# A causal mask moved from a TensorE matmul to VectorE's score copy, with three PSUM banks each for scores and transposes

## The chip, the cores and the metric

The kernel runs on one core of one Trainium2 chip. The metric is the device time of one launch in microseconds (us), as the median over runs. Engines are called PE or TensorE (matmuls), DVE or VectorE, ACT or ScalarE, POOL or GpSimd, and SP, which issues the DMAs.

## What is computed

One transformer block in fp32: adaptive layer norm, causal attention with 16 heads of 128 over 2048 tokens of 512 features, output projection and residual, then a gated feed-forward part with 4-bit weights. The change lies in attention alone:

```python
k = jnp.einsum('ihd,bpd->biph', W_K, x)     # x: the normalised, modulated input
q = jnp.einsum('ihd,bpd->biph', W_Q, x)
v = jnp.einsum('ihd,bpd->biph', W_V, x)
scores = jnp.einsum('biph,biqh->biqp', k, q)
mask = jnp.tril(jnp.ones((pos, pos), dtype=x.dtype))
masked = scores * mask - jnp.float32(10000000000.0) * (1.0 - mask)
attn = jax.nn.softmax(masked / jnp.sqrt(jnp.float32(d_head)), axis=-1)
z = jnp.einsum('biqp,biph->biqh', attn, v)
out = jnp.einsum('df,bqf->bqd', W_O, z_flat)
```

## The kernel before

Every fp32 product is made of three fp32r matmuls on split operands, hi*hi, lo*hi and hi*lo (`split_matmul`, L189 to L191); the splits are made as they are copied out of PSUM, the high part by ScalarE, the low part by VectorE. The program runs in stages with a barrier between them: `prologue` (layer norm, to 57.7 us), `attention` (58.0 to about 1701 us), `output_projection`, `gate_up`, `down`.

`attention` goes through the heads one after the other; heads 1 to 14 run in loops with one body, heads 0 and 15 are written out. A head has 16 row tiles i of 128 queries. In row i the keys come in chunks c of 512, i // 4 + 1 of them, the last as wide as the diagonal reaches (128 to 512 columns); a head has 40 chunks. The steps of a chunk, by the letters that the orders use:

- S i.c (PE, `scores`): negated and scaled scores of the chunk into a bank of `ps_s`. For the last chunk of a row a bf16 matmul against the identity adds the mask (`causal`, 128x128, a large positive number over the diagonal) to the last 128 columns (L816). The narrowest chunk, of rows 0, 4, 8 and 12, is computed 256 columns wide.
- C i.c (DVE, `copy_scores`): copy to `probs` (two rows of buffer) with the minimum of each row of the chunk; after the last chunk of a row a small reduction (L964) takes the minimum over the chunks' minima.
- E i (ACT, `exponent`): one exponential over the row with that minimum as bias, and its sum.
- T i.u (PE, `transposes`): up to four 128x128 transposes into a bank of `ps_t`. H i.u (ACT) and L i.u (DVE) copy it out as high and low parts.
- Z b.u (PE, `pv`): values times probabilities for a pair of rows; Y b (ACT) copies the result, SP stores it.
- P and U are the projections of K, Q, V and the transposition of V (W), in a single bank `ps_p`, so each must be copied out by ACT and then DVE before the next begins. N, G and R handle the reciprocals of the sums. X (DVE) and nine POOL instructions for each of three pieces a head decode the 4-bit weights in heads 0 to 10.

Three tables, `PE_ORDER`, `ACT_ORDER` and `DVE_ORDER`, set the order of these steps on the three engines by hand. A step with "-" belongs to the previous head, one with "+" to the next; the last head leaves out those with "+". Waits are semaphores: S waits until the bank it writes was copied (`row_copied`), T until its bank's low part was taken (`t_lo`), E for the row minimum. Of the eight PSUM banks, `ps_s` has 4, `ps_t` 2, `ps_z` and `ps_p` 1 each.

On POOL, `split_weights` splits the next head's weights after this head's last projection of the same kind, and in the last head `split_wo` splits W_O into the space of the normalised input, which is free once PV3 of the last head is done (`hT_used`); 16 pairs of instructions (L746, L749).

Of the kernel before, what the change touches and what calls it, by code (L numbers as in the profile page):

```python
# [136 lines left out]
PT_SLOTS = 5  # L137

# [101 lines left out]
def adaln_kernel(nc, x, w_qkv, w_o, gu_packed, gu_scales, dn_packed, dn_scales, c_cols, w_mod, out):  # L240
    with ExitStack() as whole:
# [52 lines left out]
def prologue(nc, ph, start, x, w_qkv, c_cols, w_mod, ident, ident_bf, gate_a, gate_b, shift_a, scale_a,  # L294
# [82 lines left out]
    def _(pool):  # L377
# [10 lines left out]
        pool.wait_ge(start.consts, 1)  # L388
        nc.gpsimd.affine_select(out=start.causal[:, :], in_=start.zeros[:, :], compare_op=ALU.is_ge, fill=MASKED,
# [141 lines left out]
def attention(nc, ph, start, hbm, w_qkv, w_o, gu_packed, gu_scales, dn_packed, dn_scales, ident, ident_bf,  # L531
# [16 lines left out]
    z = sb("z", [P, ZBUF, 2 * P], F32)  # L548
    cmin = sb("cmin", [P, 2, NB], F32)
# [221 lines left out]
    def _(pe):  # L771
# [29 lines left out]
        def scores(h, i, c):  # L801
# [71 lines left out]
    def _(act):  # L873
# [14 lines left out]
        def transposed_hi(h, i, u):  # L888
# [46 lines left out]
    def _(dve):  # L935
# [15 lines left out]
        def copy_scores(h, i, c):  # L951
# [7 lines left out]
            least = rmin[:, i % 2:i % 2 + 1] if nch == 1 else cmin[:, i % 2, c:c + 1]  # L959
# [554 lines left out]
```

## Time and profile before

| | |
|---|---|
| runs | 2215.63 us median of 3 (2215.61 to 2218.49) |
| profiled execution | 2216.7 us, its span 2214.6 us |
| TensorE busy | 2142.3 us (97%) |
| VectorE busy | 1333.9 us (60%) |
| ScalarE busy | 1075.6 us (49%) |
| POOL busy | 718.9 us (32%) |
| DMA | mean 55 GB/s |
| transposition of the sums' reciprocals (L853), once a head | starts at 182.4 us in the first, 1697.4 us in the last |

The profile is of one execution. A matmul's record is longer than the step from one matmul to the next, since they are pipelined: what a matmul costs in a dense stream is the distance between starts, and a busy share near 100% says only that no gap is visible. VectorE's copy with a minimum is two records: the pass and a short read of the accumulator (DVE_READ_ACCUMULATOR).

### The profile page before, as it was taken

What the parts mean: (1) busy time and instruction counts of PE and PEld (TensorE: products, weight loads), DVE (VectorE), ACT (ScalarE), POOL (GpSimd) and SP (SyncE); (2) the same over time, 40 slices, a digit from 0 to 9 for tenths busy, and PEclk for the clock granted to TensorE, in tenths of its full rate; (3) what the DMA queues carried; (4) which work ended last, traced back from release to release, by engine and by line L of the source; (5) the groups of instructions that cost most, each with busy time, mean ns of one, the idle gap of its engine ahead of it and who ended that gap; (6) DMA issues with size and microseconds to landing.
All of it is one profiled execution on the core that took longest, in us unless ns stands there. A gap on an engine that the chain in (4) does not pass through costs nothing. (4 is left out here: it accounts for less than half of the span.)

```text
span 2214.6 us, 37536 instructions
## 1 busy us (share of the span) xinstructions
PE 2142.3 (97%) x12561; PEld 1838.4 (83%) x12561; DVE 1333.9 (60%) x2998; ACT 1075.6 (49%) x2006; POOL 718.9 (32%) x545
## 2 busy tenths in 40 slices
PE   6899999999999999999999999999997899899899
PEld 3688889888888888888888888888886788788687
DVE  7364646556565646465565546464554577699865
ACT  4354545454554545454545545454544333588511
POOL 3333242525153333425250101010015444388400
PEclk9999999999999999999999999999999999999999
DMA  5111010111110110101110000000004677111121
GB/s 204 36 44 37 32 33 31 33 33 33 45 38 29 43 36 31 33 31 33 33 33 32 19 18 21 14 21 12 22 27 138 206 238 236 59 39 39 43 67 66
DMA packets 84003, 122.78 MB, mean 55 GB/s; under 512 B 9315, under 2 KB 49891, under 8 KB 83939
## 3 DMA queue, kind: packets, MB, share of 16 engines
q1 hardware_dynamic: 81635, 117.76, 16.3%
q10 hardware_dynamic: 2304, 4.20, 0.5%
q8 instruction: 36, 0.59, 0.1%
q14 instruction: 28, 0.23, 0.0%
HBM read 87.97 MB, written 33.95 MB: 55 GB/s over the span
## 5 line engine op out<-in xcount | busy, mean ns | idle before, releaser
L960 DVE TENSOR_SCALAR_CACHE_REDUCE probs<-ps_s 128x512 f32<-128x512 f32 (+3 forms) x640 | 371.2, 607 | 263.2 <-PE ps_t L827 116.4
L971 DVE TENSOR_TENSOR pT_lo<-ps_t,pT_hi 128x512 fp32r<-128x512 f32 (+3 forms) x640 | 368.9, 605 | 248.6 <-ACT pT_hi L892 247.3
L892 ACT ACTIVATE pT_hi<-ps_t 128x512 fp32r<-128x512 f32 (+3 forms) x640 | 318.6, 531 | 230.5 <-PE ps_t L827 229.6
L903 ACT ACTIVATE probs<-probs,rmin 128x128 f32<-128x128 f32 (+15 forms) x256 | 308.1, 1204 | 137.2 <-DVE rmin L964 111.9
L189 PE MATMUL ps_z<-pT_hi,v_hi 128*128 128x256 f32 (+1 forms) x1152 | 333.4, 289 | 0.0
L189 PE MATMUL ps_p<-hT_hi,w_hi 128*128 128x512 f32 x768 | 319.9, 417 | 8.7 <-PEq L269 4.1
L191 PE MATMUL ps_z<-pT_hi,v_lo 128*128 128x256 f32 (+1 forms) x1152 | 324.7, 282 | 0.0
L190 PE MATMUL ps_z<-pT_lo,v_hi 128*128 128x256 f32 (+1 forms) x1152 | 324.7, 282 | 0.0
L827 PE MATMUL ps_t<-ident,probs 128*128 128x128 f32 x2176 | 309.1, 273 | 4.5 <-DVE pT_lo L971 2.5
L191 PE MATMUL ps_p<-hT_hi,w_lo 128*128 128x512 f32 x768 | 303.1, 395 | 0.0
L190 PE MATMUL ps_p<-hT_lo,w_hi 128*128 128x512 f32 x768 | 301.1, 392 | 0.0
L827 PEld LDWEIGHTS ps_t<-ident,probs 128*128 128x128 f32 x2176 | 254.0, 140 | 39.9 <-DVE pT_lo L971 2.8
L189 PE MATMUL ps_s<-kT_hi,qT_hi 128*128 128x512 f32 (+2 forms) x640 | 262.1, 409 | 0.0
L191 PE MATMUL ps_s<-kT_hi,qT_lo 128*128 128x512 f32 (+2 forms) x640 | 233.8, 365 | 0.0
L190 PE MATMUL ps_s<-kT_lo,qT_hi 128*128 128x512 f32 (+2 forms) x640 | 233.4, 365 | 0.0
L190 PEld LDWEIGHTS ps_z<-pT_lo,v_hi 128*128 128x128 f32 x1152 | 220.2, 191 | 2.7
L189 PEld LDWEIGHTS ps_z<-pT_hi,v_hi 128*128 128x128 f32 x1152 | 220.0, 191 | 2.7
L191 PEld LDWEIGHTS ps_z<-pT_hi,v_lo 128*128 128x128 f32 x1152 | 219.7, 191 | 0.0
L233 POOL TENSOR_TENSOR w_hi<-w_raw,zeros 128x512 fp32r<-128x512 f32 x48 | 50.0, 1042 | 481.5 <-PE ps_p L191 481.5
L727 POOL TENSOR_TENSOR turn<-zeros 128x1 f32<-128x1 f32 x33 | 6.4, 193 | 552.1 <-DVE words L990 552.1
L189 PEld LDWEIGHTS ps_p<-hT_hi,w_hi 128*128 128x128 f32 x768 | 146.4, 191 | 33.2 <-issue 4.9
L191 PEld LDWEIGHTS ps_p<-hT_hi,w_lo 128*128 128x128 f32 x768 | 144.8, 189 | 33.5
(136 smaller groups left out, 3813.7 us busy)
## 6 DMA issues: line engine op xcount, KB each, us to landing
scratch_zT<-z SPq DMA_DIRECT2D x256, 64.0 KB, 1.6
o_z<-scratch_zT SPq DMA_DIRECT2D x31, 512.0 KB, 7.2
o_scales<-scratch_recips SPq DMA_DIRECT2D x31, 512.0 KB, 8.0
w_raw<-in_w_qkv SPq DMA_DIRECT2D x16, 768.0 KB, 4.5
p_wmod<-in_w_mod SPq DMA_DIRECT2D x6, 1024.0 KB, 10.6
words<-in_gu_packed SPq DMA_DIRECT2D x44, 128.0 KB, 3.1
scratch_wgu<-deq_a SPq DMA_DIRECT2D x22, 256.0 KB, 2.0
g_codes<-scratch_wgu SPq DMA_DIRECT2D x11, 512.0 KB, 3.4
```

The lines of the kernel that those rows point to most:

```text
L189: nc.tensor.matmul(dst, stat[0], mov[0], start=start, stop=False)
L190: nc.tensor.matmul(dst, stat[0], mov[1], start=False, stop=False)
L191: return nc.tensor.matmul(dst, stat[1], mov[0], start=False, stop=stop)
L233: nc.gpsimd.tensor_tensor(st.w_hi[:, m, :], st.w_raw[:, m, :], st.zeros[:, 0:1].to_broadcast([P, DC * DH]), ALU.add) \
L727: then(nc.gpsimd.tensor_tensor(turn[:, :], zeros[:, 0:1], zeros[:, 0:1], ALU.add))
L827: last = nc.tensor.transpose(ps_t[:, n % 2, (k - 4 * u) * P:(k - 4 * u + 1) * P], probs[:, i % 2, k * P:(k + 1) * P], ident[:, :])
L892: nc.scalar.activation(pT[0][:, slot, i % 2, 0:w], ps_t[:, (chunks_before(i) + u) % 2, 0:w], ACT.Copy).then_inc(t_hi, 1)
L903: nc.scalar.activation(probs[:, i % 2, 0:w], probs[:, i % 2, 0:w], ACT.Exp, bias=rmin[:, i % 2:i % 2 + 1], scale=-1.0, accum_out=sums[:, i ...
L960: nc.vector.tensor_scalar(probs[:, i % 2, c * BT:c * BT + w], ps_s[:, at % NB, 0:w], 1.0, None, ALU.mult, ALU.min, accum_out=least).then_i ...
L971: nc.vector.tensor_tensor(pT[1][:, slot, i % 2, 0:w], ps_t[:, (chunks_before(i) + u) % 2, 0:w], pT[0][:, slot, i % 2, 0:w].bitcast(F32), A ...
```

## The change

The mask matmul is gone. `causal` becomes fp32, 512 columns wide, 384 of zeros and the 128x128 mask at the end, and the last chunk of each row is copied by a `tensor_tensor_reduce`: scores plus the last w columns of `causal`, with the minimum. The row minimum is chained: each chunk's copy starts from the minimum of the one before (`least_before`), so the small reduction L964 goes, and each copy but a row's first waits for the one before it (`row_copied`). Ahead of each `tensor_tensor_reduce` stands a one-column memset (`lead`), and the waits are on it. The narrowest chunk is computed 128 wide. `ps_s` and `ps_t` have 3 banks each; a bank counter that does not divide 40 starts anew with each head (`freed`). The three orders are new.

```diff
+def freed(h, n, banks):
+
+    last = n - banks if n >= banks else max(m for m in range(CHUNKS) if m % banks == n % banks) - CHUNKS
+    return CHUNKS * h + last + 1
 PE_ORDER = """
-    S0.0 T15.2- Z7.0- T15.3- T0.0 PW0 Z7.1- Z7.2- PK1.0 PK1.1 PK1.2 PK1.3 Z7.3- N0- S1.0 S2.0 PQ1.0 PQ1.1 T1.0 PQ1.2
+    S0.0 S1.0 Z7.1- PW0 T0.0 T1.0 Z7.2- PK1.0 PK1.1 PK1.2 PK1.3 Z7.3- S2.0 N0- PQ1.0 PQ1.1 PQ1.2 PQ1.3 S3.0 Z0.0 T2.0
...
 ACT_ORDER = """
-    E0 H15.3- H0.0 UW0 UK1 G0- Y7- E1 E2 H1.0 UQ1 H2.0 Y0 E3 UV1 H3.0 UW1 E4 Y1 E5 H4.0 UK2 H4.1 H5.0 H5.1 E6 UQ2 E7
+    E0 E1 UW0 H0.0 H1.0 UK1 G0- Y7- E2 UQ1 Y0 H2.0 E3 E4 UV1 H3.0 H4.0 H4.1 UW1 Y1 E5 E6 UK2 H5.0 H5.1 H6.0 UQ2 E7 Y2
...
 DVE_ORDER = """
-    C0.0 L15.2- L15.3- L0.0 UW0 UK1 C1.0 C2.0 X0 L1.0 UQ1 L2.0 C3.0 C4.0 L3.0 UW1 C4.1 C5.0 C5.1 L4.0 C6.0
+    C0.0 C1.0 X0 UW0 L0.0 L1.0 UK1 C2.0 UQ1 C3.0 L2.0 C4.0 C4.1 L3.0 L4.0 L4.1 C5.0 C5.1 UW1 C6.0 C6.1 X1 UK2 L5.0
...
+S_BANKS = 3
+T_BANKS = 3
...
-                    causal=sb("causal", [P, P], BF16, both), zeros=sb("zeros", [P, P], F32, both),
+                    causal=sb("causal", [P, BT], F32, both), zeros=sb("zeros", [P, P], F32, both),
...
-            if not (isinstance(h, int) and CHUNKS * h + at < NB):
-                pe.wait_ge(row_copied, CHUNKS * h + at - NB + 1)
-            n = BT if c < b else max(r + 1, 2) * P
+            if not (is_at(h, 0) and at < S_BANKS):
+                pe.wait_ge(row_copied, freed(h, at, S_BANKS))
+            n = BT if c < b else (r + 1) * P
             k = [part[:, c * BT:c * BT + n] for part in kT]
-            diagonal = c == b
-            last = split_matmul(nc, ps_s[:, at % NB, 0:n], q, k, True, True)
-            if diagonal:
-                last = nc.tensor.matmul(ps_s[:, at % NB, r * P:(r + 1) * P], ident_bf[:, :], causal[:, :],
-                                        start=False, stop=True, skip_group_check=True)
-            last.then_inc(scores_ready, 1)
+            split_matmul(nc, ps_s[:, at % S_BANKS, 0:n], q, k, True, True).then_inc(scores_ready, 1)
...
-            if not (isinstance(h, int) and CHUNKS * h + n < 2):
-                pe.wait_ge(t_lo, CHUNKS * h + n - 1)
+            if not (is_at(h, 0) and n < T_BANKS):
+                pe.wait_ge(t_lo, freed(h, n, T_BANKS))
...
-            if n_chunks(i) == 1:
-                act.wait_ge(row_copied, CHUNKS * h + chunks_before(i) + 1)
-            else:
-                act.wait_ge(min_ready, (NT - TPB) * h + i - TPB + 1)
+            act.wait_ge(row_copied, CHUNKS * h + chunks_before(i + 1))
...
-            least = rmin[:, i % 2:i % 2 + 1] if nch == 1 else cmin[:, i % 2, c:c + 1]
-            nc.vector.tensor_scalar(probs[:, i % 2, c * BT:c * BT + w], ps_s[:, at % NB, 0:w], 1.0, None,
-                                    ALU.mult, ALU.min, accum_out=least).then_inc(row_copied, 1)
-            if nch > 1 and c == nch - 1:
-                dve.wait_ge(row_copied, CHUNKS * h + chunks_before(i) + nch)
-                nc.vector.tensor_reduce(rmin[:, i % 2:i % 2 + 1], cmin[:, i % 2, 0:nch], AX_X, ALU.min) \
-                  .then_inc(min_ready, 1)
+            least = rmin[:, i % 2:i % 2 + 1] if c == nch - 1 else cmin[:, i % 2, c:c + 1]
+            least_before = cmin[:, i % 2, c - 1:c] if c else None
+            if c:
+                dve.wait_ge(row_copied, CHUNKS * h + at)
+            out = probs[:, i % 2, c * BT:c * BT + w]
+            if c < nch - 1:
+                ins = nc.vector.tensor_scalar(out, ps_s[:, at % S_BANKS, 0:w], 1.0, least_before,
+                                              ALU.mult, ALU.min, accum_out=least)
+            else:
+                nc.vector.memset(lead[:, i % 2:i % 2 + 1], 0.0)
+                ins = nc.vector.tensor_tensor_reduce(out=out, in0=ps_s[:, at % S_BANKS, 0:w], in1=causal[:, BT - w:BT],
+                                                     scale=1.0, scalar=least_before if c else 3e38, op0=ALU.add, op1=ALU.min,
+                                                     accum_out=least)
+            ins.then_inc(row_copied, 1)
```

TensorE at the start of a loop head, before: S0.0 with its mask, then a bank of transposes of the previous head's last row (T15.2-) and Z7.0-.

```order
L189 MATMUL ps_s<-kT_hi,qT_hi 128x256
L190 MATMUL ps_s<-kT_lo,qT_hi 128x256
L191 MATMUL ps_s<-kT_hi,qT_lo 128x256
L816 MATMUL ps_s<-causal,ident_bf 128x128
L825 ISA
L827 MATMUL ps_t<-ident,probs 128x128 x4
L833 ISA
L837 ISA
L189 MATMUL ps_z<-pT_hi,v_hi 128x256
```

The same place of the change: S0.0 and S1.0, then Z7.1-.

```order
L197 MATMUL ps_s<-kT_hi,qT_hi 128x128
L198 MATMUL ps_s<-kT_lo,qT_hi 128x128
L199 MATMUL ps_s<-kT_hi,qT_lo 128x128
L819 REGISTER_ALU
L197 MATMUL ps_s<-kT_hi,qT_hi 128x256
L198 MATMUL ps_s<-kT_lo,qT_hi 128x256
L199 MATMUL ps_s<-kT_hi,qT_lo 128x256
L840 ISA
L841 ISA
L197 MATMUL ps_z<-pT_hi,v_hi 128x256
```

Two rows' scores now stand together at the head's start, the first of them 128 columns wide and neither with a mask matmul; T15.2- and T15.3- have moved into the head that they belong to.

TensorE at the end of row 12 in the change (S12.2, S12.3, PW3, T11.0 to T11.2, S13.0); register instructions stand between the steps.

```order
L197 MATMUL ps_s<-kT_hi,qT_hi 128x512
L198 MATMUL ps_s<-kT_lo,qT_hi 128x512
L199 MATMUL ps_s<-kT_hi,qT_lo 128x512
L819 REGISTER_ALU
L197 MATMUL ps_s<-kT_hi,qT_hi 128x128
L198 MATMUL ps_s<-kT_lo,qT_hi 128x128
L199 MATMUL ps_s<-kT_hi,qT_lo 128x128
L787 REGISTER_ALU
L796 MATMUL ps_p<-ident,vT 128x128 x4
L826 REGISTER_ALU
L831 MATMUL ps_t<-ident,probs 128x128 x12
L819 REGISTER_ALU
```

All four chunks of row 12 now follow each other, and all of row 11's transposes; before, S12.2 and S12.3 stood behind T10.2, and a projection came behind S12.3.

VectorE at the start of a loop head, before: C1.0, C2.0 and the unpacking of a weight piece (X0) come behind UK1.

```order
L948 TENSOR_TENSOR kT_lo<-ps_p,kT_hi 128x512
L957 REGISTER_ALU
L960 TENSOR_SCALAR probs,rmin<-ps_s 128x256
L957 REGISTER_ALU
L960 TENSOR_SCALAR probs,rmin<-ps_s 128x384
L984 ISA
L985 TENSOR_TENSOR words<-words,nib_shift 128x512
```

In the change (L969 is the `tensor_tensor_reduce`, its second row the read of the accumulator):

```order
L968 MEMSET lead 128x1
L969 ISA probs,rmin<-ps_s,causal 128x128
L969 ISA rmin 128x1
L957 REGISTER_ALU
L968 MEMSET lead 128x1
L969 ISA probs,rmin<-ps_s,causal 128x256
L969 ISA rmin 128x1
L991 ISA
L992 TENSOR_TENSOR words<-words,nib_shift 128x512
```

C0.0 and C1.0 open the head together, each as a memset, a masked copy and an accumulator read, and X0 is third.

## Rows read from the trace of the kernel before

**Rows 1.** windows, a loop head and the last: us, busy us by engine, granted clock, DMA.
```profile
284.02:385.59 101.57, 101.57 (x651) 89.22 (x651) 58.66 (x155) 50.87 (x97) 38.01 (x31) 1.00 0.11 35
1604.47:1697.38 92.91, 90.44 (x594) 79.33 (x594) 51.87 (x139) 48.00 (x89) 36.66 (x32) 1.00 0.17 49
```

**Rows 2.** TensorE's waits at transposes, whole run (us in total, times, longest).
```profile
PE ps_t L827 <- DVE pT_lo L971: 2.5, 4, 1.0
PE ps_t L827 <- ACT probs L903: 2.1, 1, 2.1
```

**Rows 3.** TensorE's timeline round a mask matmul with scores behind it (start, us).
```profile
1675.33 0.34 PE L191 MATMUL ps_s<-kT_hi,qT_lo 128*128 128x384 f32 x1
1675.51 0.23 PE L816 MATMUL ps_s<-causal,ident_bf 128*128 128x128 bf16 x1
1675.54 0.47 PE L189 MATMUL ps_s<-kT_hi,qT_hi 128*128 128x512 f32 x1
1675.86 0.39 PE L190 MATMUL ps_s<-kT_lo,qT_hi 128*128 128x512 f32 x1
1676.09 0.40 PE L191 MATMUL ps_s<-kT_hi,qT_lo 128*128 128x512 f32 x1
```

**Rows 4.** TensorE's timeline, a mask matmul with transposes behind it.
```profile
405.52 0.23 PE L816 MATMUL ps_s<-causal,ident_bf 128*128 128x128 bf16 x1
405.59 0.28 PE L827 MATMUL ps_t<-ident,probs 128*128 128x128 f32 x1
```

**Rows 5.** TensorE's timeline, a 256-column triple's first matmul and the mask behind it.
```profile
578.47 0.28 PE L189 MATMUL ps_s<-kT_hi,qT_hi 128*128 128x256 f32 x1
...
578.83 0.23 PE L816 MATMUL ps_s<-causal,ident_bf 128*128 128x128 bf16 x1
```

**Rows 6.** TensorE's timeline, a 128-column triple and the last matmul of attention.
```profile
1697.10 0.22 PE L189 MATMUL ps_z<-pT_hi,v_hi 128*128 128x128 f32 x1
...
1697.38 0.27 PE L853 MATMUL ps_z<-ident,recips 128*16 128x128 f32 x1
```

**Rows 7.** VectorE's groups by shape (out<-in, count, busy us, mean ns, idle before).
```profile
L971 DVE TENSOR_TENSOR pT_lo<-ps_t,pT_hi 128x512 fp32r<-128x512 f32 x448 | 296.4, 685 | 229.4 <-ACT pT_hi L892 228.2
L960 DVE TENSOR_SCALAR_CACHE_REDUCE probs<-ps_s 128x512 f32<-128x512 f32 x448 | 295.6, 687 | 170.7 <-PE ps_t L827 116.4 <-PE ps_s L191 52.3
L971 DVE TENSOR_TENSOR pT_lo<-ps_t,pT_hi 128x128 fp32r<-128x128 f32 x64 | 18.0, 282 | 2.4 <-ACT pT_hi L892 2.4
L964 DVE TENSOR_REDUCE rmin<-cmin 128x1 f32<-128x4 f32 x64 | 10.1, 157 | 2.2
```

**Rows 8.** VectorE's timeline over copies without and a reduction with an own wait.
```profile
1683.73 0.68 DVE L960 TENSOR_SCALAR_CACHE_REDUCE probs<-ps_s 128x512 f32<-128x512 f32 x1
1684.34 0.69 DVE L960 TENSOR_SCALAR_CACHE_REDUCE probs<-ps_s 128x512 f32<-128x512 f32 x1
1684.95 0.08 DVE L960 DVE_READ_ACCUMULATOR probs<-ps_s 128x1 f32 x1
1685.07 0.16 DVE L964 TENSOR_REDUCE rmin<-cmin 128x1 f32<-128x4 f32 x1
```

**Rows 9.** timeline of the first head, transposed values to the next projection.
```profile
74.00 0.60 PE L787 MATMUL ps_p<-ident,vT 128*128 128x128 f32 x4
75.26 0.69 DVE L948 TENSOR_TENSOR v_lo<-ps_p,v_hi 128x512 fp32r<-128x512 f32 x1 [0.47 <-ACT v_hi L880]
76.01 0.59 PE L189 MATMUL ps_p<-hT_hi,w_hi 128*128 128x512 f32 x1 [1.41 <-DVE v_lo L948]
```

**Rows 10.** ScalarE's group of the 256-column exponential.
```profile
L903 ACT ACTIVATE probs<-probs,rmin 128x256 f32<-128x256 f32 x16 | 8.2, 512 | 4.9 <-DVE probs L960 4.9
```

**Rows 11.** timeline, POOL's first and last W_O split, then the next stage's first load.
```profile
1651.83 1.04 POOL L746 TENSOR_TENSOR hT_hi<-w_raw,zeros 128x512 fp32r<-128x512 f32 x1 [99.23 <-PE ps_p L191]
...
1688.47 1.28 POOL L749 TENSOR_TENSOR hT_lo<-w_raw,hT_hi 128x512 fp32r<-128x512 f32 x1
...
1701.01 0.34 SPq L1085 DMA_DIRECT2D o_z<-scratch_zT  x1
```

More of the change, by code:

```diff
@@ L75 @@
-    S12.0 S12.1 T10.2 S12.2 S12.3 PQ0.0+ S13.0 T11.0 S13.1 T11.1 S13.2 S13.3 T11.2 Z5.0 S14.0 T12.0 T12.1 Z5.1 Z5.2
-    T12.2 T12.3 S14.1 S14.2 S14.3 S15.0 S15.1 S15.2 T13.0 T13.1 S15.3 PQ0.1+ PQ0.2+ PQ0.3+ T13.2 Z6.0 T13.3 PK0.0+
-    PK0.1+ PK0.2+ PK0.3+ T14.0 T14.1 Z6.1 Z6.2 T14.2 T14.3 Z6.3 PV0.0+ PV0.1+ T15.0 T15.1 PV0.2+ PV0.3+
+    S0.0 S1.0 Z7.1- PW0 T0.0 T1.0 Z7.2- PK1.0 PK1.1 PK1.2 PK1.3 Z7.3- S2.0 N0- PQ1.0 PQ1.1 PQ1.2 PQ1.3 S3.0 Z0.0 T2.0
+    S4.0 S4.1 PV1.0 PV1.1 PV1.2 PV1.3 T3.0 T4.0 T4.1 S5.0 S5.1 PW1 Z1.0 S6.0 S6.1 S7.0 PK2.0 PK2.1 PK2.2 PK2.3 T5.0
@@ new lines @@
+    T5.1 T6.0 S7.1 PQ2.0 PQ2.1 PQ2.2 PQ2.3 Z2.0 Z2.1 PV2.0 PV2.1 PV2.2 PV2.3 T6.1 T7.0 T7.1 PW2 S8.0 S8.1 S8.2 Z3.0
+    PK3.0 S9.0 S9.1 S9.2 PK3.1 Z3.1 PK3.2 PK3.3 T8.0 T8.1 T8.2 S10.0 S10.1 PQ3.0 PQ3.1 PQ3.2 PQ3.3 S10.2 T9.0 T9.1
+    T9.2 S11.0 S11.1 S11.2 Z4.0 T10.0 T10.1 T10.2 Z4.1 Z4.2 PV3.0 PV3.1 PV3.2 PV3.3 S12.0 S12.1 S12.2 S12.3 PW3 T11.0
+    T11.1 T11.2 S13.0 S13.1 S13.2 S13.3 Z5.0 T12.0 T12.1 Z5.1 Z5.2 T12.2 T12.3 T13.0 S14.0 S14.1 S14.2 PQ0.0+ PQ0.1+
+    S14.3 PQ0.2+ PQ0.3+ T13.1 T13.2 T13.3 S15.0 S15.1 S15.2 S15.3 Z6.0 Z6.1 Z6.2 T14.0 T14.1 T14.2 Z6.3 PK0.0+ PK0.1+
@@ L78 @@
+    T14.3 T15.0 T15.1 PK0.2+ PK0.3+ T15.2 T15.3 Z7.0 PV0.0+ PV0.1+ PV0.2+ PV0.3+
 """
 ACT_ORDER = """
-    E0 H15.3- H0.0 UW0 UK1 G0- Y7- E1 E2 H1.0 UQ1 H2.0 Y0 E3 UV1 H3.0 UW1 E4 Y1 E5 H4.0 UK2 H4.1 H5.0 H5.1 E6 UQ2 E7
-    H6.0 Y2 H6.1 UV2 H7.0 H7.1 UW2 Y3 UK3 E8 E9 UQ3 H8.0 H8.1 UV3 H8.2 H9.0 UW3 H9.1 H9.2 E10 H10.0 H10.1 Y4 E11
-    H10.2 H11.0 E12 H11.1 H11.2 H12.0 H12.1 E13 Y5 H12.2 H12.3 E14 H13.0 H13.1 UQ0+ H13.2 H13.3 UK0+ H14.0 H14.1
-    E15 H14.2 H14.3 Y6 H15.0 H15.1 UV0+ H15.2
+    E0 E1 UW0 H0.0 H1.0 UK1 G0- Y7- E2 UQ1 Y0 H2.0 E3 E4 UV1 H3.0 H4.0 H4.1 UW1 Y1 E5 E6 UK2 H5.0 H5.1 H6.0 UQ2 E7 Y2
@@ L88 @@
-    L8.0 L8.1 C10.0 C10.1 L8.2 L9.0 UW3 C10.2 C11.0 L9.1 L9.2 X2 C11.1 C11.2 L10.0 L10.1 C12.0 C12.1 C12.2 C12.3
-    L10.2 L11.0 C13.0 L11.1 L11.2 C13.1 C13.2 L12.0 L12.1 C13.3 C14.0 C14.1 C14.2 C14.3 L12.2 L12.3 L13.0
-    L13.1 UQ0+ L13.2 C15.0 L13.3 C15.1 C15.2 C15.3 UK0+ L14.0 L14.1 R0 L14.2 L14.3 L15.0 L15.1
+    C0.0 C1.0 X0 UW0 L0.0 L1.0 UK1 C2.0 UQ1 C3.0 L2.0 C4.0 C4.1 L3.0 L4.0 L4.1 C5.0 C5.1 UW1 C6.0 C6.1 X1 UK2 L5.0
+    L5.1 L6.0 C7.0 C7.1 UQ2 L6.1 L7.0 UW2 L7.1 C8.0 C8.1 C8.2 C9.0 C9.1 C9.2 X2 UK3 L8.0 L8.1 L8.2 C10.0 C10.1 C10.2
@@ L91 @@
+    UQ3 L9.0 C11.0 C11.1 L9.1 L9.2 C11.2 L10.0 L10.1 L10.2 C12.0 C12.1 C12.2 C12.3 UW3 L11.0 C13.0 C13.1 C13.2 L11.1
+    L11.2 C13.3 L12.0 L12.1 L12.2 L12.3 L13.0 C14.0 C14.1 C14.2 C14.3 C15.0 L13.1 L13.2 L13.3 C15.1 C15.2 C15.3 UQ0+
+    R0 L14.0 L14.1 L14.2 L14.3 L15.0 L15.1 UK0+ L15.2 L15.3
 """
@@ L387, in _ @@
         nc.gpsimd.memset(start.zeros[:, :], 0.0).then_inc(start.consts, 1)
[L388 to L389 removed]
+        nc.gpsimd.memset(start.causal[:, 0:BT - P], 0.0).then_inc(start.consts, 1)
+        pool.wait_ge(start.consts, 2)
+        nc.gpsimd.affine_select(out=start.causal[:, BT - P:BT], in_=start.zeros[:, :], compare_op=ALU.is_ge, fill=MASKED,
                                 base=0, pattern=[[-1, P]], channel_multiplier=1).then_inc(start.consts, 1)
```

24 lines of the change are left out of this document (11 added, 13 removed).

## Prediction

> **What bounds the kernel now.** I read the page's first part, then the windows of single heads, then the waits of TensorE, then its timeline. The windows show a head as a fixed period: 101.57 us, of which TensorE is busy 101.57, VectorE 58.66, ScalarE 50.87, POOL 38.01, at a granted clock of 1.00, the upper of the two levels (2.4 GHz) [rows 1]. A busy share alone could hide short waits. The waits say that there are none in the loop: at transposes TensorE waited 4.6 us in the whole run, five times, once in the first head and four times in the last [rows 2], whose window has 90.44 busy of 92.91 us [rows 1]. So in heads 1 to 14 time is the sum of the distances between matmul starts. What leaves that stream is gained, and what VectorE takes on costs nothing until TensorE has to wait for it. The other stages have no edit.
>
> **What leaves TensorE.** *The mask matmul.* Its record says 0.23 us, which is not its cost. With scores behind it: from L191 at 1675.33 to the second matmul of the next step at 1675.86 are 0.53 us [rows 3]. Without it these would be 0.18 (a 384-column matmul to what follows it) and 0.23 (512 columns, 1675.86 to 1676.09), 0.41 together. The mask costs 0.12 us. With a transpose behind it, it costs its own step, 0.07 us [rows 4]. By the order before, 11 of the 16 in a head are followed by fp32r matmuls and 5 by transposes (rows 0, 6, 7, 10, 13): 11 x 0.12 + 5 x 0.07 = 1.67 us a head.
>
> *The narrower chunk.* A 256-column triple takes 0.36 us (578.47 to 578.83) [rows 5], one of 128 columns 0.28 (1697.10 to 1697.38, the same split matmuls in Z) [rows 6]. Four rows a head: 0.32 us. The Trainium skill, "TensorE: Matmul & The Clock Gate", section "Back-to-back issue gap", gives N/2.4 + 2.5 ns for a warm matmul, thus 0.056 us for 128 columns and 0.109 for 256, and by it the saving would be 0.16 us a triple, 0.64 a head. The section on LDWEIGHTS of that page gives 0.107 us for a load of 128 columns, which would hold a narrow matmul up, and the row's 0.28 for three goes with this. I take the row.
>
> Together 1.99 us a head. All 16 heads have the same 16 masks and four narrow chunks: 31.8 us. The other matmuls are the same in number and width; their new order costs nothing by itself, since a change from transposes to fp32r matmuls moves a start but not the sum of two steps.
>
> **What VectorE takes on.** The trace has no `tensor_tensor_reduce`. The nearest rows are L971, two inputs, one in PSUM and one in SBUF, 685 ns for 512 columns and 282 for 128, and L960, one input with a minimum, 687 for 512 [rows 7]. They agree, so I price the new one like them, nothing on top. Below that it can't go, as no VectorE row that reads PSUM is faster; above, see the rivals. The memset has one column: between the accumulator read, 0.08 us, and L964, 0.16 [rows 7, 8]; I take 0.1, 16 times 1.6 us. Chaining costs overlap: copies that wait for nothing start 0.61 us apart (1683.73, 1684.34), while an instruction that waits for the copy before it starts 0.73 behind it (1685.07) [rows 8], so 24 chained copies cost up to 24 x 0.12 = 2.9 us. Twelve L964 go; behind one the next instruction would have followed some 0.2 us sooner: 2.2 us. VectorE ends near 61 us of a head of 99.6. The sum is hidden by TensorE; only its place in the order could matter.
>
> **Where TensorE could now wait.** I laid the new orders out with the steps above and looked at the short distances.
>
> (a) Head start. From S0.0: S0.0 0.28, S1.0 0.36, Z7.1 four triples 1.44, PW0 four transposes of 0.11 (0.60 for four records, 0.27 for one [rows 6, 9]) to 2.52, T0.0, T1.0 at 2.63. E1 must be done by then. S1.0 ends near 0.8, its copy near 1.4 with memset and read, E1 takes 0.51 [rows 10] behind E0: about 2.05. Slack 0.58. PK1.0 wants to start at 2.63 + 0.22 + 1.44 = 4.29; from the start of PW to the next projection are 2.01 us (74.00 to 76.01, ScalarE and VectorE both free) [rows 9], so 2.08 + 2.01 = 4.09. Slack 0.20.
>
> (b) S12.3 with three banks reuses that of S12.0 and comes after S12.0 to S12.2, 3 x 0.69 = 2.08. The copy C12.0 starts near 0.9, and is done at 1.65. Slack 0.4; S13.3 and S15.3 have the same distance. Ahead of C13.0 VectorE has C12.1 to C12.3 (0.73 each, the last narrow), UW3 and L11.0: it starts near 4.85 and ends at 5.6, and S13.3 is due at 2.08 + 0.28 + 0.44 + 12 x 0.11 + 2.08 = 6.2. Slack 0.57. With two banks for transposes the order before had to keep such distances there; a third loosens them.
>
> (c) Last head. POOL's splits of W_O start when PV3 is through and take 1651.83 to 1689.75, 37.9 us; TensorE ends at 1697.4 and the next stage begins at 1701.01, 3.6 later [rows 6, 11]. In the new order PV3 comes later: behind it TensorE has rows 12 to 15, transposes of rows 11 to 15, Z5 to Z7 and PW3, 33.2 us, and waits as before for want of the next head's projections (T14.3 behind E15, T15.2 and T15.3), 3.3. So the next stage is due 36.5 + 3.6 = 40.1 after PV3, POOL is done at 38. Cover shrinks from 11 to 2 us and still holds; without it each us would show once. I put the changes of both written-out heads at nothing, within 1 us.
>
> No slack is negative, so the steady head is 101.57 - 1.99 = 99.6.
>
> **The sum.** The profiled execution took 2216.7 us, its span 2214.6. 2216.7 - 31.8 = 2184.9. The median of the runs is 1.1 below the profiled one: 2184.
>
> **Rivals.**
>
> *Half rate.* The Trainium skill, "Vector Engine (DVE) Microarchitecture Reference", section "Points that are easy to get wrong", says that a two-source operation with an accumulator halves its throughput if both sources are in SBUF and not bf16. Here one is in PSUM, and L971 shows no loss [rows 7], but L971 accumulates nothing. As a mechanism: the slope of L971 is (685 - 282) / 384 = 1.05 ns a column, so half rate adds 0.13 us at 128 columns and 0.54 at 512. At (a) that is 0.13 + 0.27 against 0.58, at (b) 0.13 against 0.57. Only small waits come of it, 0 to 0.5 us a head: 2184 to 2192. Chance 0.12.
>
> *Waits of queues.* My distances are estimates of some 0.2 us, and (a) has that much. Three to five places late by 0.1 to 0.2 give up to 0.8 us a head: to 2196. Chance 0.13. If instead the new order lost all that the matmuls gave, 1.7 to 2.3 us a head, the time would be within 2211 to 2220. For it speaks that ScalarE and VectorE now meet longer runs of scores and transposes; against it, VectorE's 39 us of room a head. Chance 0.05.
>
> *A dear reduce (slower).* `tensor_tensor_reduce` is no row here, and could have a fixed price F on top. At the head's start two stand in line: 2F - 0.58 us lost; at (b) F - 0.57. Both reach the 1.99 gained at F = 1.05. At 1.5 a head loses 3.35, net 1.36, and the time is 2215.6 + 16 x 1.36 = 2237. Against it: the shortest VectorE rows, 0.08 and 0.16 us [rows 7, 8], leave no room for a fixed microsecond in what that engine does here. Chance 0.05.
>
> **How the numbers follow.** The likeliest case, 0.65, is 2184 within 2180 (all 16 masks worth 0.12, and no waits in the first head's start) and 2188. Half rate and small waits add 0.25 up to 2196. The range 2180 to 2196 leaves out 0.1. Faster by over 0.2% (4.4 us, about what a measurement of this kernel tells from no change): 0.90; within it 0.05; slower 0.05.
>
> **What would show it.** The last matmul of two following heads should stand 99.6 us apart, with TensorE's starts 0.23 apart from the last chunk's third matmul to the next step. L969 should read near 0.69 us for 512 columns, the memset 0.1, a chained copy start 0.73 behind the one before. TensorE's waits in the loop should be none; those for `ps_s` would be new, and so would POOL as the last before the next stage. The prediction is wrong if the windows of single heads show TensorE less than busy, above all at T1.0, PK1.0 or S13.3, or if L969 has a price of its own.

## The result, and the profile after

The changed kernel takes 2183.13 us (median of 4 runs, 2178.68 to 2183.67), the kernel before 2215.62 (median of 4, 2212.49 to 2218.49). The ratio is 0.9849, 95% interval 0.9831 to 0.9868: 1.5% faster. The forecast was 2184 within 2180 to 2196. The profiled execution took 2183.67 us, its span 2181.7.

The windows of a loop head and of the last head, cut as in [rows 1] from one transposition of the reciprocals to the next, columns as there:

```profile
core 0: us, PE busy (x) PEld busy (x) DVE busy (x) ACT busy (x) POOL busy (x), PEclk, DMA share, GB/s
280.09:379.59 99.50, 99.50 (x635) 89.51 (x633) 59.79 (x158) 49.94 (x97) 38.00 (x32) 1.00 0.11 36
...
1573.59:1664.43 90.84, 88.90 (x570) 79.89 (x569) 51.86 (x137) 45.95 (x86) 35.98 (x32) 0.98 0.18 50
```

A loop head went from 101.57 to 99.50 us, 2.07 less, and TensorE still has no gap in it. Fourteen of them give 29.0 us, the last head 2.1 (92.91 to 90.84), the first 1.4 (124.44 to 123.08), and attention begins 0.5 sooner. That is 33.0, and the spans differ by 32.9.

In the loop it does not matter where in a head the mark stands; in the two written-out heads it does. The new order has S1.0, S2.0 and T1.0 ahead of the mark (N0-), the old one behind it. TensorE's timeline at the start of the last head's window, before and after:

```profile
1604.47 0.27 PE L853 MATMUL ps_z<-ident,recips 128*16 128x128 f32 x1
1604.50 0.36 PE L189 MATMUL ps_s<-kT_hi,qT_hi 128*128 128x256 f32 x1
...
1605.62 0.47 PE L189 MATMUL ps_p<-hT_hi,w_hi 128*128 128x512 f32 x1
```

```profile
1573.02 0.39 PE L197 MATMUL ps_s<-kT_hi,qT_hi 128*128 128x384 f32 x1
...
1573.59 0.27 PE L857 MATMUL ps_z<-ident,recips 128*16 128x128 f32 x1
1573.61 0.48 PE L197 MATMUL ps_p<-hT_hi,w_hi 128*128 128x512 f32 x1
```

S1.0 and S2.0 took 1.12 us there, T1.0 some 0.2 more: about 1.3 us of work moved from the last window into the first. Neither 2.1 nor 1.4 can be read alone. Their sum can: the two heads gave 3.4 us together, where the forecast had 4.0.

TensorE's waits inside attention, the whole run. Between 183 and 1573 us the list is empty.

```profile
PE ps_p L197 <- DVE kT_lo L948: 2.3, 2, 1.4
PE ps_t L831 <- DVE pT_lo L978: 1.6, 1, 1.6
PE ps_p L197 <- DVE qT_lo L945: 1.5, 1, 1.5
PE ps_t L831 <- ACT probs L903: 1.3, 2, 1.2
PE ps_p L197 <- DVE v_lo L948: 0.8, 1, 0.8
PE ps_s L197 <- DVE probs L965: 0.2, 1, 0.2
```

All are in the two written-out heads, as in [rows 2]. The wait on a bank of scores (`ps_s`) is new and is 0.2 us in the last head. The four waits on `pT_lo` of the last head have become one of 1.6.

VectorE's groups in the loop head, by shape (names, shapes, count, busy us, mean ns, idle before), to read beside [rows 7]:

```profile
L965 DVE TENSOR_SCALAR_CACHE_REDUCE probs<-ps_s,cmin 128x512 f32<-128x512 f32 x12 | 9.0, 750 | 1.4
L965 DVE TENSOR_SCALAR_CACHE_REDUCE probs<-ps_s 128x512 f32<-128x512 f32 x12 | 8.2, 686 | 5.6 <-PE ps_s L199 5.5
...
L969 DVE CUSTOM_DVE_ANT_0 probs<-ps_s,causal,cmin 128x512 f32<-128x512 f32 x3 | 2.2, 750 | 0.0
...
L969 DVE CUSTOM_DVE_ANT_0 probs<-ps_s,causal,cmin 128x128 f32<-128x128 f32 x3 | 1.1, 351 | 0.0
...
L968 DVE MEMSET lead<- 128x1 f32 x16 | 0.9, 59 | 1.2
L969 DVE CUSTOM_DVE_ANT_0 probs<-ps_s,causal 128x512 f32<-128x512 f32 x1 | 0.7, 685 | 0.0
...
L969 DVE CUSTOM_DVE_ANT_0 probs<-ps_s,causal 128x128 f32<-128x128 f32 x1 | 0.3, 287 | 2.8 <-issue 2.8
```

The reader is to compare rows with and without `cmin` among the inputs. Without it the new reduce takes 685 ns for 512 columns and 287 for 128, which is what L971 took. With it, the chained minimum as its start, both the plain copy and the reduce take 64 to 65 ns more. In VectorE's timeline two chained copies in a row (start, us) stand 0.88 apart, where unchained ones stand 0.61 apart [rows 8]:

```profile
348.52 0.75 DVE L965 TENSOR_SCALAR_CACHE_REDUCE probs<-ps_s,cmin 128x512 f32<-128x512 f32 x1
...
349.40 0.75 DVE L965 TENSOR_SCALAR_CACHE_REDUCE probs<-ps_s,cmin 128x512 f32<-128x512 f32 x1
```

### The profile page after: what moved, and what is told of

The parts are those of the page before. It is cut to its first block and busy times, and to the rows that moved or that the text cites. A ratio compares the mean times of both kernels' runs of the same rounds, so it can differ in the third digit from the quotient of the medians.

```text
span 2181.7 us, 37262 instructions
## 1 busy us (share of the span) xinstructions
PE 2112.4 (97%) x12305; PEld 1845.1 (85%) x12305; DVE 1353.7 (62%) x3062; ACT 1059.6 (49%) x2006; POOL 719.3 (33%) x546
## 5 line engine op out<-in xcount | busy, mean ns | idle before, releaser
L978 DVE TENSOR_TENSOR pT_lo<-ps_t,pT_hi 128x512 fp32r<-128x512 f32 (+3 forms) x640 | 360.3, 605 | 219.9 <-ACT pT_hi L895 219.7
L895 ACT ACTIVATE pT_hi<-ps_t 128x512 fp32r<-128x512 f32 (+3 forms) x640 | 304.9, 534 | 87.5 <-PE ps_t L831 86.2
L197 PE MATMUL ps_z<-pT_hi,v_hi 128*128 128x256 f32 (+1 forms) x1152 | 326.4, 283 | 0.0
L197 PE MATMUL ps_p<-hT_hi,w_hi 128*128 128x512 f32 x768 | 309.6, 403 | 8.6 <-PEq L277 4.1
L831 PE MATMUL ps_t<-ident,probs 128*128 128x128 f32 x2176 | 278.9, 274 | 3.1 <-DVE pT_lo L978 1.6
L197 PE MATMUL ps_s<-kT_hi,qT_hi 128*128 128x512 f32 (+3 forms) x640 | 244.1, 381 | 0.2 <-DVE probs L965 0.2
L199 PE MATMUL ps_s<-kT_hi,qT_lo 128*128 128x512 f32 (+3 forms) x640 | 233.1, 364 | 0.0
L198 PE MATMUL ps_s<-kT_lo,qT_hi 128*128 128x512 f32 (+3 forms) x640 | 232.7, 364 | 0.0
L965 DVE TENSOR_SCALAR_CACHE_REDUCE probs<-ps_s 128x512 f32<-128x512 f32 x192 | 131.7, 686 | 88.4 <-PE ps_s L199 87.0
L198 PEld LDWEIGHTS ps_p<-hT_lo,w_hi 128*128 128x128 f32 x768 | 145.7, 190 | 24.3
```

What stands on the lines that cost most here:

```text
L197: nc.tensor.matmul(dst, stat[0], mov[0], start=start, stop=False)
L198: nc.tensor.matmul(dst, stat[0], mov[1], start=False, stop=False)
L199: return nc.tensor.matmul(dst, stat[1], mov[0], start=False, stop=stop)
L831: last = nc.tensor.transpose(ps_t[:, n % T_BANKS, (k - 4 * u) * P:(k - 4 * u + 1) * P], probs[:, i % 2, k * P:(k + 1) * P], ident[:, :])
L965: ins = nc.vector.tensor_scalar(out, ps_s[:, at % S_BANKS, 0:w], 1.0, least_before, ALU.mult, ALU.min, accum_out=least)
L978: nc.vector.tensor_tensor(pT[1][:, slot, i % 2, 0:w], ps_t[:, (chunks_before(i) + u) % T_BANKS, 0:w], pT[0][:, slot, i % 2, 0:w].bitcast(F ...
```

## The experiments

Loop heads are read as periods between the reciprocals' transpositions; inside one profile nearly all repeat within some 0.05 us, and two profiles of the changed kernel have 99.50 and 99.47, so a single profile resolves what a median of whole runs does not.

### Taking the parts of the change apart

**The mask matmul alone, in the old orders.** Nothing takes its place, so the diagonal blocks stay unmasked.

```diff
-            if diagonal:
-                last = nc.tensor.matmul(ps_s[...], ident_bf[:, :], causal[:, :], start=False, stop=True, ...)
```

> The kernel before with the 16 mask matmuls of a head left out and nothing put in their place, so that the diagonal blocks are not masked; everything else, the orders and the 4 and 2 banks too, stays. My theory: a mask matmul costs TensorE 0.12 us ahead of scores or projections and 0.07 ahead of transposes, 11 and 5 times a head, 1.67 us. The loop head goes from 101.57 to 99.90, the time by 26.7 us to 2189. Rival one: the cost is the 0.23 us of its record, 3.7 us a head: 97.9 and 2157. Rival two: it costs only its 128 columns at the full clock, 0.056 us, 0.9 a head: 100.7 and 2201. If the changed kernel owes something to its orders beyond the instructions, this run and the wide-chunk run together explain less than the 2.07 us a head that it gained.

Measured: 2187.54 us (2184.54 to 2190.30), ratio 0.9873 [0.9853, 0.9892]. A loop head:

```profile
282.60:382.33 99.73, 99.73 (x636) 89.00 (x635) 58.50 (x155) 50.84 (x97) 38.10 (x31) 1.00 0.11 36
```

The mask costs 1.84 us a head in the old orders, 0.115 us each over all 16, where 1.67 was expected. Neither rival holds (3.7 and 0.9).

**The narrow chunk undone.**

```diff
-            n = BT if c < b else (r + 1) * P
+            n = BT if c < b else max(r + 1, 2) * P
```

> The changed kernel with one part undone: the last chunk of scores is again at least 256 columns wide (four rows a head). My theory: 0.08 us a triple of matmuls, 0.32 a head; the loop head goes from 99.50 to 99.82, the time by 5.1 us to 2188. Rival: time of a triple in proportion to its columns, 0.16 us each, 0.64 a head: 100.14 and 2193. If nothing changes (99.50), TensorE is not what sets the head at these places.

Measured: 2184.72 us (2184.11 to 2186.55), ratio 0.9862 [0.9845, 0.9879]. The narrow chunk is worth 0.17 us a head and not 0.32. A loop head:

```profile
282.49:382.16 99.67, 99.67 (x635) 89.66 (x634) 59.81 (x158) 49.92 (x97) 38.02 (x32) 1.00 0.11 36
```

TensorE's timeline shows where the rest went. First the changed kernel, row 8's last chunk and the Z behind it, then the same place with 256 columns:

```profile
309.42 0.22 PE L197 MATMUL ps_s<-kT_hi,qT_hi 128*128 128x128 f32 x1
309.48 0.28 PE L198 MATMUL ps_s<-kT_lo,qT_hi 128*128 128x128 f32 x1
309.59 0.27 PE L199 MATMUL ps_s<-kT_hi,qT_lo 128*128 128x128 f32 x1
309.70 0.33 PE L197 MATMUL ps_z<-pT_hi,v_hi 128*128 128x256 f32 x1
309.87 0.28 PE L198 MATMUL ps_z<-pT_lo,v_hi 128*128 128x256 f32 x1
```

```profile
311.88 0.28 PE L197 MATMUL ps_s<-kT_hi,qT_hi 128*128 128x256 f32 x1
311.99 0.28 PE L198 MATMUL ps_s<-kT_lo,qT_hi 128*128 128x256 f32 x1
312.11 0.28 PE L199 MATMUL ps_s<-kT_hi,qT_lo 128*128 128x256 f32 x1
312.23 0.28 PE L197 MATMUL ps_z<-pT_hi,v_hi 128*128 128x256 f32 x1
312.35 0.28 PE L198 MATMUL ps_z<-pT_lo,v_hi 128*128 128x256 f32 x1
```

The triple itself went from 0.35 to 0.28 us, as forecast. But the first matmul behind a narrow triple keeps its place for 0.17 us instead of 0.12. From the first score matmul to the second Z matmul are 0.45 us against 0.47: most of the gain of the triple is given back one step later.

**Orders and banks alone, under the old instructions.**

The kernel before, with the changed kernel's `PE_ORDER`, `ACT_ORDER` and `DVE_ORDER`, `S_BANKS = 3`, `T_BANKS = 3` and `freed`.

> The kernel before (mask matmul on TensorE, minimum by a reduction of its own, last chunk at least 256 wide) with only the three new orders and the 3 and 3 banks. The old orders under the changed instructions gave a loop head of 100.32 us with two waits of 0.29 and 0.33 us at transposes. My theory now: those waits come from the shorter TensorE stream against two banks for transposes; the orders give nothing to the old instructions except some 12 fewer changes between transposes and fp32r matmuls at about 5 ns. Loop head 101.45 to 101.55, time 2213 to 2216. Rival: the orders are worth 0.8 us a head whatever the instructions: 100.75, time 2203. Third: the old instructions wait in the new orders, loop head over 101.7.

Measured: 2209.52 us (2208.15 to 2212.54, 10 runs), ratio 0.9978 [0.9969, 0.9987]. A loop head:

```profile
284.09:385.41 101.32, 101.32 (x651) 89.77 (x651) 58.86 (x154) 49.95 (x97) 37.98 (x32) 1.00 0.11 35
```

With the old instructions the orders give 0.25 us a head; the expectation was 0.06 from fewer changes between transposes and fp32r steps, the rival 0.8. No wait was removed (there was none before), so it is the sum of the distances that shrank. The new order has 121 distances from transpose to transpose in a head instead of 109, thus 12 changes fewer. But those changes are not what the 0.25 is made of. The two runs without the mask, this section's first (99.73) and the one with the wide chunk (99.67), have the same 634 matmuls a head, one in the old order and one in the new, and neither has a wait in the loop, so their different work on VectorE is hidden. Between them the orders give 0.06 us, 0.005 for each of the 12 changes. The other 0.19 is there only while the mask matmuls are: with them 101.57 to 101.32, without 99.73 to 99.67. The masks as a whole cost 1.84 us in the old order and 1.65 in the new. What makes this difference stays open; by the prediction's prices the new order, with 12 masks ahead of fp32r matmuls and 4 ahead of transposes instead of 11 and 5, would cost 0.05 more.

The last head's window fell from 92.91 to 89.95. About 1.3 of these 2.96 us are the steps that stand ahead of the mark now (592 matmuls in the window before, 582 here), and TensorE's gaps in it fell from 2.5 to 1.0.

**The new instructions in the old orders, with 4 and 2 banks.**

> The changed kernel with the three orders of before and with the banks of before (4 for scores, 2 for transposed chunks); mask on VectorE, chained minimum and 128-column chunk stay. My theory: the gain comes from the instructions that leave TensorE, the orders give nothing by themselves, so the loop head is 99.50 to 99.7 and the time 2180 to 2188. Rival: with two banks for transposed chunks and VectorE's new work in the old places, TensorE waits somewhere in each head, and the new orders are what keeps the gain: loop head 100 to 101.6, time 2191 to 2216. The waits of TensorE in the loop (none, or at scores or transposes) tell them apart.

Measured: 2196.77 us (2196.31 to 2199.87), ratio 0.9919 [0.9901, 0.9937]. The rival holds. Window, TensorE's waits from 200 to 1500 us, then VectorE's and TensorE's timelines at one of the two places:

```profile
282.68:383.00 100.32, 100.02 (x635) 88.75 (x635) 59.25 (x159) 50.89 (x97) 38.09 (x31) 1.00 0.11 35
```

```profile
PE ps_t L831 <- DVE pT_lo L978: 2.6, 14, 0.3
```

```profile
339.29 0.69 DVE L965 TENSOR_SCALAR_CACHE_REDUCE probs<-ps_s 128x512 f32<-128x512 f32 x1 [0.88 <-PE ps_t L831]
...
340.12 0.75 DVE L965 TENSOR_SCALAR_CACHE_REDUCE probs<-ps_s,cmin 128x512 f32<-128x512 f32 x1
...
341.01 0.75 DVE L965 TENSOR_SCALAR_CACHE_REDUCE probs<-ps_s,cmin 128x512 f32<-128x512 f32 x1
...
341.94 0.35 DVE L969 CUSTOM_DVE_ANT_0 probs<-ps_s,causal,cmin 128x128 f32<-128x128 f32 x1
...
342.22 0.55 DVE L978 TENSOR_TENSOR pT_lo<-ps_t,pT_hi 128x384 fp32r<-128x384 f32 x1
```

```profile
342.31 0.40 PE L199 MATMUL ps_s<-kT_hi,qT_lo 128*128 128x512 f32 x1
342.83 0.33 PE L831 MATMUL ps_t<-ident,probs 128*128 128x128 f32 x1
```

The matmul at 342.31 is followed by a transpose 0.52 us later instead of 0.23: 0.29 lost, and 0.33 at a second place. (The list of waits has less, 0.19 a head: it counts a gap only from the modelled end of the matmul before it.) The transpose waits for L978 at 342.22, which frees one of only two banks and stands behind four copies of row 12 in line. With starts 0.83 to 0.93 apart they hold VectorE for 2.9 us; with the unchained 0.61 I estimate 0.8 less. The run without the mask has the same orders and banks and unchained copies, and no wait in the loop. So what made the wait is VectorE's new work against the two banks. That most of it is the chain is the estimate just made; no run has the old orders with unchained copies. The new orders and the third bank take the wait away: 100.32 to 99.50, 0.82 us a head, 0.62 of it these two places.

Two further combinations, 3 and 3 banks under the old orders and 4 and 2 under the new, were not tried, since the engines would wait for each other for ever. Under the old orders with 3 banks for scores S15.3 waits for C15.0, which VectorE has behind L13.2, whose transposes TensorE has behind S15.3. Under the new orders with 2 banks T13.3 waits for L13.1, which VectorE has behind C15.0, whose scores TensorE has behind T13.3.

**The chain undone, in the new orders.**

```diff
-            ins = nc.vector.tensor_scalar(out, ps_s[...], 1.0, least_before, ...)   # and a wait for the copy before
+            ins = nc.vector.tensor_scalar(out, ps_s[...], 1.0, None, ...)
+            nc.vector.tensor_reduce(rmin[...], cmin[:, i % 2, 0:nch], AX_X, ALU.min)   # once a row, 12 a head
```

> The changed kernel with the chain undone: each copy takes its own minimum, without a pointer to the one before and without the wait for it, and the small reduction over the minima (0.16 us) is back for 12 rows a head. My theory: the chain is hidden either way. The loop head stays 99.50, the time within 2 us of 2183. VectorE's busy time goes from 59.79 by 24 times 0.065 less and 12 times 0.16 more to about 60.1. Rival: the chain shortens or lengthens the way from scores to the exponent at a place where TensorE stands close behind: loop head off 99.50 by 0.1 or more, with a wait at transposes.

Measured: 2180.83 us (2179.57 to 2183.37), ratio 0.9841 [0.9824, 0.9857]; loop head 99.49 in the first two, 99.47 in the rest. The chain gives the loop nothing. VectorE's busy time fell to 58.95 us, not rose to 60.1: unchained copies overlap each other's ends and chained ones do not. The last head took 88.67 us: with copies that take less time E15 starts 76.40 us into it and not 77.55 (1652.11 less 1575.71, 1651.14 less 1573.59), and the wait at T14.3 shrank from 1.6 to 0.5. Of the 2.17 us between 90.84 and 88.67 that is half; the other 1.06 is the clock, which was at its upper level here and in a second profile of the changed kernel too, whose last head took 89.78 with the wait as long (below). The medians of this and the changed kernel (2180.83, 2183.13) are no further apart than single runs of one of them.

### How much room the new orders leave

**More VectorE time ahead of each masked copy: an instruction more.** A memset of 256 columns, then of 800, then of 1, each into a tile that nothing reads.

```diff
                 nc.vector.memset(lead[:, i % 2:i % 2 + 1], 0.0)
+                nc.vector.memset(spare[:, i % 2, 0:256], 0.0)      # 0:800 in the second
```

> The changed kernel with one more VectorE instruction ahead of each masked copy (16 a head): a memset of 256 columns that nothing needs. By the memset of one column (0.06 us) and some 1.05 ns a column I estimate it at 0.33 us. It stands for a fixed price of 0.33 us on each masked copy. By the slacks of the prediction (twice the price less 0.58 at the head's start, once less 0.57 at S13.3) nothing or 0.1 us shows: loop head 99.5 to 99.6. Rival: each masked copy lies on the way that sets TensorE's pace, and 16 times 0.33 shows as 5.3 us a head.

> The same with a memset of 800 columns, estimated at 0.9 us. By the same two slacks: 1.2 us lost at the head's start and 0.3 at S13.3, loop head 101.0 (100.5 to 101.6), so nearly the whole gain is gone, and the waits stand at T1.0 (or PK1.0) and S13.3 or near it. Rivals: the slacks are larger and it stays under 100; or further places give way and it is over 102.

> The changed kernel with one more VectorE instruction ahead of each masked copy, of one column (0.06 us), so that their number is that of the 256-column run and their time next to nothing. There, VectorE stood 1.2 to 1.5 us with nothing to wait for at the start of each head whose loop body also holds the dequantisation's steps, and the loop head was 100.4 to 100.7 us; in the others it was 99.5. Theory one: what matters is how many instructions the loop body holds, so the same stall is there and the loop head in these heads is 100.4 or more, 99.5 in the others. Theory two: the stall came of the time that the memset took; then it is 99.5 in all heads.

Measured, one profile each: with 256 columns (0.27 us each) 2194.67 us, loop heads 100.4 to 100.8 at the starts of heads 2 to 10 and 99.5 in the others; with 800 columns (0.725) 2220.95 us, 101.9 to 102.2 (one 103.9) and 101.1; with 1 column (0.06) 2193.75 us, 100.3 to 100.8 and 99.5. The expectation for 256 columns (99.5 to 99.6) held in the second loop and missed by 1 us in the nine heads at whose start the first loop jumps back; that for 800 (101.0) held in the second loop too, within 0.1. The 1-column run settles it: what costs 1.1 us in nine heads is not the time of the memsets. Its VectorE timeline at the start of head 2, and the last score matmul that the copy needs:

```profile
273.77 0.06 DVE L969 MEMSET lead<- 128x1 f32 x1 [2.85 <-PE ps_s L199]
273.78 0.06 DVE L970 MEMSET spare<- 128x1 f32 x1
275.82 0.29 DVE L971 CUSTOM_DVE_ANT_0 probs<-ps_s,causal 128x128 f32<-128x128 f32 x1 [1.98 <-issue]
```

```profile
273.43 0.27 PE L199 MATMUL ps_s<-kT_hi,qT_lo 128*128 128x128 f32 x1
```

The scores are there at 273.7, two memsets run, and the next instruction comes 1.98 us late with nothing to wait for. The page's queue of VectorE's instructions says what it lacked (packets, MB, share), first the changed kernel, then the one with 16 short instructions more:

```profile
q14 instruction: 29, 0.24, 0.0%
```

```profile
q14 instruction: 75, 0.61, 0.1%
```

46 packets more: five for each of the nine times that the first loop jumps back (heads 1 to 10, whose body also holds the decoding of weights), and one. One of them lands between 274.0 and 274.6. In the changed kernel 4 packets move on that queue in the first pass of the loop (180 to 280 us) and none in the next (280 to 380), as if the body were held from then on. The Trainium skill, "Runtime: NRT & Kernel Launch", section "Instruction fetch mechanics", states the mechanism: a taken branch whose target is not in the small window of held instructions forces a fetch before execution goes on. The trace agrees, in that the packets and the standing come together and behind the jump, and puts 1.98 us on it here. The edge lies between the unchained kernel (29 packets) and this one (75), and the second loop, which has fewer instructions, stays on the near side in all. That q14 is VectorE's I take from its count following VectorE's body alone.

**The same time without an instruction more.**

```diff
-                nc.vector.memset(lead[:, i % 2:i % 2 + 1], 0.0)
+                nc.vector.memset(lead[:, i % 2, :], 0.0)           # lead is 800 wide
```

> The changed kernel with its own memset ahead of each masked copy widened from 1 to 800 columns: no instruction more, 0.67 us more for each masked copy. In the run with an extra memset of 800 columns (0.73 us) the loop head was 102.0 us in heads with dequantisation steps and 101.1 in the others. Theory one (the number of instructions made the 0.9 us between them): now both kinds of heads are near 101.0, with waits at T1.0, at another transpose and at S13.3. Theory two (time alone did it): 102 and 101 again. By the prediction's slacks alone it would be 99.50 + 0.75 + 0.10 = 100.35 in all.

Measured: 2209.34 us in one profile, 29 packets, and a loop head of 101.01 to 101.09 in both loops:

```profile
284.84:385.85 101.01, 100.29 (x635) 89.36 (x633) 67.73 (x158) 50.25 (x97) 37.97 (x32) 1.00 0.11 35
```

Theory one holds. 0.67 us on each masked copy costs 1.5 us a head. Laid beside the changed kernel matmul by matmul, the loss stands at three places, with 0.09 at a fourth (T12.0): T1.0 0.76, which is the 2F - 0.58 of the prediction to the hundredth; S13.3 0.32, where it said 0.10; and T4.0 0.35, which it did not have. So the price at which the gain is gone is below the 1.05 us of the prediction, near 0.8 by my estimate, if the three go on growing by 4 us for each us of F (2 at T1.0, 1 at each of the others).

### The last head

**Orders of its own for the last head, with the chain and without; the changed kernel again beside them.**

```diff
+PE_LAST = reordered(PE_ORDER, "Z6.0 Z6.1 Z6.2 T14.0 T14.1 T14.2 Z6.3 PK0.0+ PK0.1+ T14.3",
+                    "Z6.0 T14.0 Z6.1 T14.1 Z6.2 T14.2 Z6.3 T14.3")
+ACT_LAST = reordered(ACT_ORDER, "E15 H14.0 H14.1 H14.2 Y6", "H14.0 H14.1 H14.2 E15 Y6")
+DVE_LAST = reordered(DVE_ORDER, "R0 L14.0 L14.1 L14.2", "L14.0 L14.1 L14.2 R0")
```

> The changed kernel; only the written-out last head has orders of its own: row 14's transposed chunks go ahead of E15 on ScalarE and ahead of the reciprocal on VectorE, and Z6 lies between T14's chunks. My theory: T14.3 no longer waits 1.6 us, T15.0 waits 0.4 at most, and the clock, which stood at its lower level for 3.4 us behind that wait, stays at the upper one. Last head from 90.84 to about 88.2, loop heads 99.50 as they are, time 2180.5. Rival: the work put ahead of E15 delays it, the wait moves to T15.0 whole, and the last head keeps 90 or more with the clock falling there too.

> The last-head orders together with the unchained minimum, which alone had a last head of 88.67 us against 90.84, since E15 and H14 came 0.9 us sooner. My theory: both shorten the way to T15.0, the gains do not add: last head 87.5 to 88.2, time 2180. Rival: the unchained minimum already took all there was, 88.6, and 2181. A fall of the clock behind a wait of under 0.7 us would speak against a link of the two.

> The changed kernel once more beside the three others, for the comparison of some 2 us: 2183, last head 90.8 with a wait of 1.6 us and a stretch at the lower clock behind it. If that stretch is absent here, the clock falls by chance and not behind the wait.

Measured: 2182.52 us (2178.89 to 2183.69), 2182.66 (2179.73 to 2184.68) and 2181.40 (2177.43 to 2184.03), ratios 0.9851, 0.9852 and 0.9851, each within 0.0016: no difference. The last heads took 90.84, 89.52 and 89.78. For the new last orders alone my theory fell and its rival held: the wait moved whole from T14.3 to T15.0, as this row of that run shows.

```profile
1656.17 1.09 PE L843 MATMUL ps_t<-ident,probs 128*128 128x128 f32 x8 [1.67 <-ACT probs L915]
```

With the unchained minimum too, neither the theory (87.5 to 88.2) nor the rival (88.6) held: 89.52, with a wait of 1.68 at T15.0 and the clock at its upper level, so these last orders took away 0.85 of what the unchained minimum alone had reached (88.67).

The clock did not go with the wait. Windows of 6 us from around the wait, of the changed kernel's first profile and of its second:

```profile
1654.00:1660.00 6.00, 5.37 (x30) 4.64 (x31) 4.87 (x8) 3.85 (x8) 5.76 (x6) 0.72 0.48 119
```

```profile
1653.70:1659.70 6.00, 5.01 (x39) 4.35 (x40) 4.74 (x8) 3.71 (x8) 5.77 (x6) 1.00 0.46 117
```

The same kernel with the same wait of 1.63 us had the lower level (1.2 GHz) for a part of the window once and not the other time, which is the 1.06 us between 90.84 and 89.78. Of seven profiles of these runs with one wait of 1.6 to 1.8 us in the last head, three had the fall; of two with a wait of 2.3 us (0.67 us more on each masked copy, and the extra 800 columns) the first had it and the second not. What decides it stays open. None of these beats the changed kernel by what can be measured.

## Why the prediction was right, step by step

- **What bounds.** Right: the loop has no wait of TensorE before or after, and the head's period is the sum of the distances between starts.
- **The mask, 1.67 us a head.** In the new orders it is 101.32 less 99.67, which is 1.65 (between these two runs VectorE's work differs too, hidden); in the old orders 1.84. The term held within a tenth, and why the two differ is not shown.
- **The narrow chunk, 0.32.** Over-sized: 0.17. I priced the triple alone, and the step behind it gives part back. The formula that I had weighed, of the Trainium skill, "TensorE: Matmul & The Clock Gate", section "Back-to-back issue gap" (0.64 by it), was further off; the section gives it for a matmul by itself and not for a stream with weight loads.
- **"Their new order costs nothing by itself."** It gains a little: 0.06 us a head where no mask matmul is in the stream, 0.25 where the masks are. The statement that a change of kind "moves a start but not the sum" held within 0.005 us a change.
- **The sum.** Masks out in the old order 1.84, new order 0.06, narrow chunk 0.17: 2.07 against 1.99. With the orders first it reads 0.25, 1.65 and 0.17. Either way 0.15 too much for the chunk is made up by some 0.2 that the forecast did not have, so the loop head hit more closely than its terms, and that is luck.
- **VectorE's price.** The reduce priced like L971: exact without the chain (685), 65 ns short with it. The memset is 0.06, not 0.1. A chained copy starts 0.88 behind the one before, not 0.73, so the chain costs 0.27 where I had 0.12. Busy 59.8 of 99.5, near 61 of 99.6 forecast. All of it hidden in the new orders; in the old ones it is what makes TensorE wait.
- **Slacks.** (a) at T1.0 as forecast to 0.01, closer than the 0.2 that I gave such distances; PK1.0 did not give way; (b) tighter by 0.2; T4.0 was missing. None negative, as said.
- **Written-out heads.** Forecast 4.0 us for the two, measured 3.4, so "nothing, within 1 us" held, but as a net sum. In the last head TensorE's gaps are 1.9 us (90.84 less 88.90) against 2.5; the forecast had put them at 3.3, though [rows 1] have 2.5. A stretch at the lower clock cost 1.1. What took the rest is not shown. POOL's W_O splits ended 0.6 us after TensorE (1665.07 against 1664.43), and the next stage's first load came at 1668.08, 3.65 after TensorE's last transposition: the shrunk cover held.
- **Rivals.** Half rate: excluded, (685 - 287) / 384 = 1.04 ns a column. Waits of queues: none in the loop here, and real under the old orders (0.6 us a head), which I had not asked of the old table. Dear reduce: no.

## What to carry to other kernels

When an engine with a dense stream loses instructions, price them by distances between starts and include the step behind: the next instruction can give half of it back. Work that another engine takes over is free only by its place: here the same instructions cost 0.8 us a head more in the old order, though VectorE idles 40% of the time. Before adding instructions to a loop body, look at the engine's instruction queue in the page: here it moved nothing in the loop's later passes until 16 tiny instructions more made it move, and these cost more than their whole time.

## What was not expected of the hardware

- 16 instructions of 0.06 us in a loop body made VectorE stand 1.5 to 2.0 us at each jump back, with 5 instruction packets a pass where there were none; 1.1 us of it reached the time.
- A row minimum as a start value (a [128, 1] operand) adds 64 to 65 ns to a copy with accumulator, at 128 columns as at 512, and with the wait for it moves starts from 0.61 to 0.88 us.
- Behind a triple of 128-column fp32r matmuls the next matmul's distance is 0.17 us instead of 0.12.
- The granted clock fell to its lower level behind a wait of 1.6 us in one profile of a kernel, and not in the next profile of the same kernel.
- Sixteen mask matmuls a head cost 1.84 us in one order of the same stream and 1.65 in another, with no wait in either.
